# Zeros behind the rows of a sparse expert layer: eight tiles per group, or two row buffers filled once

## What is computed

```python
x = x + attn_a(layernorm(x))   # delta rule, 16 heads of 8, short convolutions
x = x + ffn(layernorm(x))      # 8 experts, the best 2 of each token
x = x + attn_b(layernorm(x))   # linear attention, 16 heads of 8
x = x + ffn(layernorm(x))      # the same experts again
```

```python
probs = softmax(xt @ Wg); topw, topi = top_k(probs, 2); topw = topw / sum(topw)
h = relu(einsum('nd,edf->enf', xt, W1)); y = einsum('enf,efd->end', h, W2)
out = einsum('ne,end->nd', combine, y)   # combine holds topw at topi, else 0
```

## Time and profile before

| | us |
|---|---|
| median of 3 runs | 790.13 |
| lowest and highest | 786.14, 790.35 |
| span of the profiled execution | 951.4 |

### The profile page before, as it was taken

The page is one execution under the profiler, slowest core; times in us unless marked ns, Lnnn a source line. Parts: engine busy times, 40 slices in busy tenths (PEclk is TensorE's granted clock), DMA queues, the critical chain, the costliest instruction groups (busy, mean ns, idle before and its releaser), DMA issues.

```text
span 951.4 us, 17059 instructions
## 1 busy us (share of the span) xinstructions
PE 722.5 (76%) x5202; PEld 588.9 (62%) x5202; DVE 620.4 (65%) x1684; ACT 482.5 (51%) x1270; POOL 479.8 (50%) x550
## 2 busy tenths in 40 slices
PE   5634649888889877878979975798887988199375
PEld 4322428767677756665867865685655868188364
DVE  4789999999999999995754753464434626033224
ACT  4965476979796846474540613243241704054221
POOL 2149896989898989477042033303341122702351
PEclk9865668999999989899875995798777959589697
DMA  5330403040403030103333222234122414335321
GB/s 181 81 81 0 103 11 104 12 114 12 113 11 102 11 103 12 56 1 94 91 97 92 90 68 84 62 89 129 45 87 84 121 45 139 98 101 156 114 73 45
DMA packets 106766, 73.99 MB, mean 78 GB/s; under 512 B 44992, under 2 KB 94656, under 8 KB 106432
## 3 DMA queue, kind: packets, MB, share of 16 engines
q1 hardware_dynamic: 102080, 63.58, 22.8%
q0 software_dynamic: 4608, 9.45, 3.3%
HBM read 45.47 MB, written 27.53 MB: 77 GB/s over the span
## 4 chain that ended last, share of the span: by engine, by line
PE 39%; DVE 27%; issue 13%; another core or an unknown queue 8%; ACT 6%; DMA 3%; POOL 2%; SPq 1%; DVEq 0%; POOLq 0%; ACTq 0%
PE bank L2036 7%; DVE u L2578 6%; PE bank L2122 5%; PE bank L2101 5%; PE bank L2002 5%; DVE hist_mem L2583 4%; DVE hist_mem L2587 4%; DVE prod_mem L2571 3%; PE bank L2092 2%; PE bank L2052 2%; DVE x L2719 2%; PE bank L2040 1%; DMA s_beta<-beta_T 1%; PE bank L1745 1%
## 5 line engine op out<-in xcount | busy, mean ns | idle before, releaser
L1836 PE MATMUL bank<-w,hid 128*128 128x128 f32 x768 | 105.8, 296 | 32.9 <-DVE y_even L2719 17.9
L1836 PEld LDWEIGHTS bank<-w,hid 128*128 128x128 f32 x768 | 99.8, 209 | 44.5 <-issue 13.3
L885 POOL TENSOR_TENSOR oq_mem<-hist_mem,q_t 128x384 f32<-128x384 f32 (+1 forms) x96 | 101.3, 1089 | 0.0
L2578 DVE TENSOR_REDUCE u<-prod_mem 128x32 f32<-128x288 f32 x128 | 86.8, 678 | 3.4
L1175 ACT ACTIVATE hid<-bank 128x512 f32<-128x512 f32 x112 | 62.7, 594 | 50.2 <-PE bank L1816 35.2
L2122 PE MATMUL bank<-w,wv 128*128 x448 | 70.9, 308 | 21.1 <-issue 16.9
L2036 PEld LDWEIGHTS bank<-v_bd,hist_mem 128*64 128x64 f32 x1024 | 74.0, 167 | 17.3 <-issue 17.0
L2036 PE MATMUL bank<-v_bd,hist_mem 128*64 128x18 f32 x1024 | 77.1, 233 | 5.2 <-issue 5.2
L953 POOL DMA_INDIRECT s_xs<-xf,row_at x40 | 39.5, 988 | 81.8 <-DVE row_at L3043 38.1
L2122 PEld LDWEIGHTS bank<-w,wv 128*128 128x128 f32 x448 | 63.8, 218 | 26.3 <-issue 26.1
L1347 ACT ACTIVATE wv<-bank 128x512 f32<-128x512 f32 x56 | 33.7, 602 | 83.7 <-remote 48.6
(11 more groups left out here) (303 smaller groups left out, 1948.6 us busy)
## 6 DMA issues: line engine op xcount, KB each, us to landing
hid<-in_w SPq DMA_DIRECT2D x72, 128.0 KB
s_qkv<-qkv SPq DMA_DIRECT2D x24, 256.0 KB, 3.4
pin<-s_xs SPq DMA_DIRECT2D x76, 64.0 KB
pin<-s_qkv SPq DMA_DIRECT2D x16, 256.0 KB, 2.6
kk<-in_w SPq DMA_DIRECT2D x30, 128.0 KB
s_ys<-q_p SPq DMA_DIRECT2D x28, 128.0 KB
s_ys<-q_t SPq DMA_DIRECT2D x28, 128.0 KB
s_xs<-zeros SPq DMA_DIRECT2D x40, 64.0 KB
```

The lines of the kernel that those rows point to most:

```text
L885: tt(oq[:, :, j, :, 0:HD], s_at, bc(turned[:, n, j], 2, HD), ALU.mult).then_inc(o_part, 1)
L1836: last = nc.tensor.matmul(bank[:, y_bank(e, wide), tokens], hid[:, e % 2, f, tokens], w2[:, e, f], start=(f == 0), stop=(f == FC - 1))
L2578: red(u[:, n], prod[:, n].rearrange("p m e j -> p m j e"), AX_X, ALU.add).then_inc(step, 1)
```

## The change

The group's own row buffers give way to two, `s_rows[0]` and `s_rows[1]`, each large enough for the largest group; group g uses number g % 2. SP fills both with zeros once, in the first layer: sixteen DMAs out of `state`, which is still zero then, four in each of the iterations 0 to 3, as the last thing of the iteration. A tile that reaches past an expert's rows therefore holds zeros, or finite rows that an earlier group left there. `pads` goes, and with it the tile `zeros`, the table of counts `pad_at`, the cast that writes it, and SP's wait for the pads.

Three waits are added. GpSimd's first scatter and VectorE's first sum into `state` wait until all fills have landed. The scatters of groups 2, 3 and 4 wait until TensorE has turned every pair of the groups up to g - 2, the earlier user of the same buffer.

```diff
-        s_xs = [nc.dram_tensor(f"s_xs{g}", [E * ROOM[g], D], F32, kind="Internal").ap() for g in range(len(GROUPS))]
+        s_rows = [nc.dram_tensor(f"s_rows{b}", [E * max(ROOM), D], F32, kind="Internal").ap() for b in range(2)]
+        s_xs = [s_rows[g % 2][0:E * ROOM[g]] for g in range(len(GROUPS))]
...
-        CONSTS, SELECT_OPS, TABLE_OPS = 6 + 2 * len(GROUPS), 8, 20
+        CONSTS, SELECT_OPS, TABLE_OPS = 5 + 2 * len(GROUPS), 8, 19
+        FILLS, FILL_STEPS = E * max(ROOM) * D // (128 * B * H * HV), 4
...
+            def zero_rows(i):
+
+                count = 2 * FILLS // FILL_STEPS
+                for k in range(count * i, count * (i + 1)):
+                    b, at = k // FILLS, k % FILLS
+                    sp.dma_start(s_rows[b].rearrange("(n p q) d -> n p (q d)", n=FILLS, p=128)[at],
+                                 state[:].rearrange("p b h e -> p (b h e)")).then_inc(zeroed, 16)
+
+            sp.wait_ge(pool_ready, POOL_ALL)
             for i in range(NCH - 1):
...
                 if far:
                     load_x(i + 4)
+                if i < FILL_STEPS:
+                    zero_rows(i)
...
-            def pads(g):
-
-                sp.wait_ge(tabled, TABLE_OPS * g + 17)
-                _, starts_at = nc.values_load_multi_w_load_instructions(
-                    pad_at[0:1, g], engines=[mybir.EngineType.SP], min_val=0, max_val=E * ROOM[g] - TILE,
-                    skip_runtime_bounds_check_because=ROWS_WHY)
-                for e in range(E):
-                    sp.dma_start(s_xs[g][bass.ds(starts_at[e], TILE)], zeros[:]).then_inc(padded, 16)
-
             def tile_load(p):
...
-                sp.wait_ge(tabled, TABLE_OPS * g + 17)
+                sp.wait_ge(tabled, TABLE_OPS * g + 16)
...
-                    sp.wait_ge(padded, 16 * E * (g + 1))
...
-            pads(0)
             tile_load(0)
...
-            nc.gpsimd.memset(zeros[:], 0.0).then_inc(consts, 1)
...
                 pool.wait_ge(o_part, NG * GROUP_OPS * NCH)
+                if k == 0:
+                    pool.wait_ge(zeroed, 16 * 2 * FILLS)
+                if g >= 2:
+                    pool.wait_ge(tile_turned, FIRST_TILE[g - 1] // 2)
...
                     dve.wait_ge(numer, J * (c + 1))
+                    if c == 0:
+                        dve.wait_ge(zeroed, 16 * 2 * FILLS)
                     tt(state[:], state[:], dstate, ALU.add).then_inc(state_ready, 1)
...
                 tt(counts, count_at, expert_at[:, g], ALU.subtract).then_inc(tabled, 1)
-                nc.vector.tensor_copy(pad_at[:, g], count_at[one]).then_inc(tabled, 1)
```

More of the change, by code:

```diff
@@ L221, in build @@
         every = sb("every", [128, 128])
-        zeros = sb("zeros", [128, D])
         tile_steps = sb("tile_steps", [128, max(ROOM) // TILE])
@@ L250, in build @@
                  ("started", MOST_TILES * E), ("tile_row", MOST_TILES), ("tile_table", len(GROUPS) * MOST_TILES * 2),
-                 ("pad_at", len(GROUPS) * E), ("tiles", 2 * E), ("first", MOST_TILES), ("expert", MOST_TILES),
+                 ("tiles", 2 * E), ("first", MOST_TILES), ("expert", MOST_TILES),
                  ("offset", MOST_TILES), ("counts", E), ("shift", E)]
@@ L262, in build @@
         tiles, starting, shift = low["tiles"][:, 0:E], low["tiles"][:, E:2 * E], low["shift"]
-        pad_at = low["pad_at"][0:1].bitcast(I32).rearrange("p (g k) -> p g k", g=len(GROUPS))
         BUFFERS = 6
-        ROWS_WHY = "a tile starts inside its expert's room, and a pad starts at an expert's count, which is less than the room by a tile"
+        ROWS_WHY = "a tile starts inside its expert's room"
         EXPERT_WHY = "a tile's expert is the number of experts, of seven, whose tiles start at or below it"
@@ L355, in build @@
         selected, positioned, rows_ready, route_part = sem("selected"), sem("positioned"), sem("rows_ready"), sem("route_part")
-        tabled, padded, combined = sem("tabled"), sem("padded"), sem("combined")
+        tabled, zeroed, combined = sem("tabled"), sem("zeroed"), sem("combined")
         mid_stored, out_stored = sem("mid_stored"), sem("out_stored")
@@ L660, in _ @@
             tile_load(7)
-            pads(1)
             tile_load(8)
@@ L686, in _ @@
             tile_store(13)
-            pads(2)
             tile_load(20)
@@ L713, in _ @@
             tile_load(31)
-            pads(3)
             tile_store(24)
@@ L738, in _ @@
             tile_load(43)
-            pads(4)
             tile_store(35)
@@ L2013, in routed_away @@
                 if full:
-                    pe.wait_ge(tabled, TABLE_OPS * (full - 1) + 2)
+                    pe.wait_ge(tabled, TABLE_OPS * (full - 1) + 1)
             def lin_numer(c, j):
@@ L2106, in tile_up @@
                 k = 2 * p - FIRST_TILE[g]
-                pe.wait_ge(tabled, TABLE_OPS * g + 17)
+                pe.wait_ge(tabled, TABLE_OPS * g + 16)
                 _, experts[p] = nc.values_load_multi_w_load_instructions(
@@ L3067, in table @@
                 tt(counts, count_at, expert_at[:, g], ALU.subtract).then_inc(tabled, 1)
-                nc.vector.tensor_copy(pad_at[:, g], count_at[one]).then_inc(tabled, 1)
                 dve.wait_ge(tabled, base + 1)
                 tt(past[:, :, 0:steps], bc(counts, 2, steps), bc(tile_steps[:, 0:steps], 1, E), ALU.is_gt).then_inc(tabled, 1)
+                dve.wait_ge(tabled, base + 2)
+                red(tiles, past[:, :, 0:steps], AX_X, ALU.add).then_inc(tabled, 1)
                 dve.wait_ge(tabled, base + 3)
-                red(tiles, past[:, :, 0:steps], AX_X, ALU.add).then_inc(tabled, 1)
+                tt(starts, bc(tiles, 1, E), lower[:], ALU.mult).then_inc(tabled, 1)
@@ L3073, in table @@
                 dve.wait_ge(tabled, base + 4)
-                tt(starts, bc(tiles, 1, E), lower[:], ALU.mult).then_inc(tabled, 1)
+                red(starting, starts, AX_X, ALU.add).then_inc(tabled, 1)
                 dve.wait_ge(tabled, base + 5)
-                red(starting, starts, AX_X, ALU.add).then_inc(tabled, 1)
-                dve.wait_ge(tabled, base + 6)
                 tt(started[:, 0:many], bc(number, 2, E), bc(starting[one], 1, many), ALU.is_ge).then_inc(tabled, 1)
                 red(total[:], low["tiles"][one, E - 1:2 * E:E], AX_X, ALU.add).then_inc(tabled, 1)
-                dve.wait_ge(tabled, base + 8)
+                dve.wait_ge(tabled, base + 7)
@@ L3087, in table @@
                 red(first, started[:, 0:many], AX_X, ALU.max).then_inc(tabled, 1)
+                dve.wait_ge(tabled, base + 12)
+                tt(offset, number, first, ALU.subtract).then_inc(tabled, 1)
                 dve.wait_ge(tabled, base + 13)
-                tt(offset, number, first, ALU.subtract).then_inc(tabled, 1)
+                stt(tile_row[:, 0:many], offset, float(TILE), tile_row[:, 0:many], ALU.mult, ALU.mult).then_inc(tabled, 1)
                 dve.wait_ge(tabled, base + 14)
-                stt(tile_row[:, 0:many], offset, float(TILE), tile_row[:, 0:many], ALU.mult, ALU.mult).then_inc(tabled, 1)
@@ L3092, in table @@
-                dve.wait_ge(tabled, base + 15)
                 stt(tile_table[:, g, 0:many, 0], expert, float(ROOM[g]), tile_row[:, 0:many], ALU.mult, ALU.add).then_inc(tabled, 1)
@@ L3099, in back @@
                 rows_of = slice(0, 2 * J * count)
-                dve.wait_ge(tabled, TABLE_OPS * g + 17)
+                dve.wait_ge(tabled, TABLE_OPS * g + 16)
                 dve.wait_ge(route_part, 4 * (k + count))
@@ L3103, in back @@
                    bc(shift, 1, 2 * J * count), ALU.mult).then_inc(tabled, 1)
+                dve.wait_ge(tabled, TABLE_OPS * g + 17)
+                red(row_shift[:, rows_of], sel_shift[:, rows_of], AX_X, ALU.add).then_inc(tabled, 1)
                 dve.wait_ge(tabled, TABLE_OPS * g + 18)
-                red(row_shift[:, rows_of], sel_shift[:, rows_of], AX_X, ALU.add).then_inc(tabled, 1)
-                dve.wait_ge(tabled, TABLE_OPS * g + 19)
                 tt(back_at[:, k:k + count].rearrange("p c s j -> p (c s j)"), row_sum[:, 0:count].rearrange("p c s j -> p (c s j)"),
```

4 lines of the change are left out of this document (2 added, 2 removed).

## The result

| | before | after |
|---|---|---|
| median (lowest to highest), us | 790.24 (786.14 to 799.63), 4 runs | 805.76 (804.09 to 806.66), 4 runs |
| first layer ends at, us in the trace | 435.73 | 456.51 |
| VectorE's waits at `kdot`, us | 3.5 | 22.3 |
| GpSimd's waits for `beta_p`, us | 30.8 | 50.8 |

The changed kernel is slower: ratio 1.0215, 95% interval 1.0181 to 1.0249, so 17 us (14.3 to 19.7). "First layer ends" is the start of its last sum into `o_p` on VectorE. The profiled execution of after took 804.9 us, close to its timed runs; that of before took 951.4 us, and the first experiment shows where the difference lies.

What follows compares the result with a forecast made beforehand. VectorE was taken to bound the first layer, TensorE being busiest in the second. Fills cost 22.3 us, less 2 for pads and 0.3 for casts: +20 us, 790.1 + 20 = 810 us, range 804 to 818, widened 795 to 826.

Steps and rivals of the forecast that it cites:

- The fills stand between s_beta's landing and beta_p's load, and small DMAs wait for them: First layer, SP's queue, chunks 2 to 5: fills priced at their full data time ahead of the pairs.
- Rival B: First layer: small loads overtake the fills or slip between them, only 2 us of gain left, 788 us; chance 0.12.
- 6.55 us a step: First layer: data time of a step's four fills, 2.36 MB at the 360 GB/s of earlier loads.
- Rival C: First layer: stores slower than loads, a step over 10 us; 832 us at 12 us, 863 at the upper bound; chance 0.10.
- the prediction's own formula: First layer: four steps of fill time, less 3.0 us of empty queue and 0.9 us of slack at chunk 5.
- the prediction's 22.3 us: First layer: total cost of the fills, 26.2 less 3.0 less 0.9 us.
- The signs to look for: Changed trace: `kdot` idle 5 to 7 us in chunks 2 to 5, `pairs_in` landing in 8 to 9, first layer ending about 457.
- Pads: 2 us: Second layer: gain from dropping SP's forty pad stores put at 2 us, between 0 and 34.3.
- The margin of 5 to 6 us: Second layer, after `pads(3)`: spare time between the group's first load and TensorE's turn of that tile pair, pads included.
- rival D: Second layer: SP paces it and pads lie on the path; gain up to 34.3 us, time 778, faster from 22.3; chance 0.08.
- The waits added for the shared buffers, and the cast: Second layer: scatter waits cost nothing (tightest margin 13 us, group 3); dropping five casts counted as 0.3 us gained.
- The 161 us between trace and timed runs: Traced span 951.4 against 790.1 us: difference placed in the second layer, the first layer's 22.3 us carried over unscaled.

Runs made afterwards that it cites:

- the first experiment: The kernel before, unchanged, profiled once more: one run of 803.68 us, span 802.0 us.
- fills_after_xr: The changed kernel with each step's four fills moved to the next iteration, behind `load_xr`: 784.27 us, ratio 0.9917 to the kernel before.
- fills_after_pairs: The changed kernel with the fills moved one place, right behind `pairs_in` of the next iteration: 798.44 us, ratio 1.0127 to the kernel before.
- before_again: The kernel before, unchanged, in its second profile: one run of 803.68 us, first layer ending at 436.32 us.
- fills_only: The kernel before, pads kept, plus the sixteen fills at the change's place into two buffers nobody reads: 814.84 us, ratio 1.0298 to the kernel before.
- fills_half: `fills_only` with each fill half as wide (128 x 2304 B): 969.03 us where the kernel before takes 957.04, ratio 1.0142.
- pads_full_2: `fills_after_xr` with the pads and their table entry put back and one more SP wait, rerun on a third chip: 794.03 us, ratio 1.0037 to before.
- fills_after_xr_2: `fills_after_xr` run again on the third chip, as control without pads: 784.33 us, ratio 0.9912 to the kernel before.

## Why the prediction was right

The forecast was 810 us against 805.76 measured, with the sign and the place right. By its own steps:

- *The fills stand between s_beta's landing and beta_p's load, and small DMAs wait for them.* Right: `fills_after_xr` and `fills_after_pairs` have the same traffic and lose nothing, or lose it elsewhere. Rival B, hidden fills, is out. The row that it was read from was thin evidence, though: a 64 KB load issued at 4.11 us, ahead of the 1 MB load, took 4.5 us to land too, so the 5.1 us of the 0.5 KB load don't single out the large one.

```profile
prod_mem<-in_wbeta SPq DMA_DIRECT2D x1, 64.0 KB, 4.5
```

- *6.55 us a step.* Too high: the row taken was that of loads at 360 GB/s, and the fills moved 423 GB/s, 5.6 us a step. Rival C, slow stores, is out by the same rows. With 5.6 us the prediction's own formula gives 4 x 5.6 - 3.0 - 0.9 = 18.5 us, and the waits at `kdot` grew by 18.8. The first layer as a whole grew by 20.2 us (against `before_again`) to 20.8 (against the trace of before); the 1.4 to 2 us that aren't at `kdot` I didn't follow up. By the timed runs the fills at this place cost 23.5 us (`fills_only` against before, and the change against `fills_after_xr`), so the prediction's 22.3 us is near the whole price by luck: too much for the waits it describes, and nothing for another 2 to 4 us, which no run here places and which are no wider than the intervals. The Trainium skill, "DMA: Bandwidth & Descriptors" (section "Anatomy of one DMA — SWDGE (gpsimd) path"), with its 436 GB/s gave an estimate of 5.4 us a step where the fixed part overlaps; its fit is for DMAs from GpSimd and these come from SP, but the trace's 5.6 us agrees with it better than with my row. The 50 us that it gave with the fixed part not overlapped are far from what was measured, and `fills_half` shows a price that follows the bytes.
- *The signs to look for.* `kdot` in chunks 2 to 5: 5.63, 5.27, 4.55, 4.43 us where 5 to 7 were expected, none in later steps. The first layer ends at 456.5 us (457 forecast). One sign was wrong: `pairs_in` was to be issued at the same place and to land in 8 to 9 us. At chunk 2 it was issued 2.2 us later, because the four fills took SP 3.38 us to issue, some 0.85 us each and not 0.4, and its loads landed in 3.9 to 4.0 us (median). The delay is the same, split between issue and landing. That is not harmless: SP's other issues are held too, and that the issue of the fills adds nothing of its own holds only as far as what followed had to wait for their data anyway.
- *Pads: 2 us.* Mis-sized. They were worth 6.5 to 9.7 us by three comparisons (`fills_only` with after, `fills_after_xr` with before, `pads_full_2` with `fills_after_xr_2`), the last of them with the reserve told above. The margin of 5 to 6 us was argued at the first load of one group, from the trace of a chip whose second layer takes 516 us where it takes 356 to 366 with pads on the others; and it left out the loads of `x_b` and the stores behind the pads, and what a gap costs TensorE in clock. This is a piece of rival D: pads on the path, but far from the 22.3 us from which it would decide. D took SP's time for the pads to be the same in the timed runs as in the trace; it wasn't. The five groups take SP 34.3 us there and 21.2 us in `before_again` (3.96, 4.65, 4.61, 4.00 and 3.99), so all of it could not have given 22.3.
- *The waits added for the shared buffers, and the cast.* No wait of theirs shows up: GpSimd's longest wait ahead of a scatter, 17.8 us, is for `row_at`, as in the earlier trace rows, and the next, 17.0 us, is the same in `before_again`.
- *The 161 us between trace and timed runs.* Right to look for them in the second layer, and to carry the first over unscaled: it ends at 435.7 us in one trace and 436.3 in the other.

Put together with what was measured: 790.2 + 23.5 - 6.5 = 807.2 us by the timed runs, and 790.2 + 20.5 - 6.5 = 804.2 with what the first layer shows, against 805.76. The forecast was 4.2 us too high. Most of that is the pads, put at 2 us (2.3 with the cast) and worth at least 6.5; the rest is within the intervals. Its range of 804 to 818 is wider at the top than its own terms make it: fills of 17 to 27 us less 2.3 give 804.8 to 814.8, and the result lies in both.

## What to carry to other kernels

Large transfers that nobody waits for belong at the place in a queue's order where the next small transfer is far off, not where the loop happens to end: here the same 9.4 MB cost 20 us of the first layer in one place and nothing four or five calls further on. Before a DMA is placed, read what is issued behind it on its queue and who waits for that, and price it as its bytes over the rate that large transfers reach. The price of a short stall of TensorE can be the stall and a stretch at the lower clock behind it, so that small delays on a DMA queue in a TensorE-bound stage can be worth more than their own length. Forty small issues that looked like free work were worth 6.5 to 9.7 us here, and an eighth of their bytes cost the same.

## What the hardware showed beyond that

- *SP's issue time isn't constant.* The two `pin` issues take 0.80 us before, 1.33 us behind four half fills and 2.34 us behind four whole ones (chunk 2); a fill's own issue took 0.43 to 1.25 us in the trace of after.
- *These stores are faster than the first loads.* 421 to 425 GB/s at a share of 1.03 to 1.04 with rows of 4608 B and 408 at 1.04 with rows of 2304 B, against 360 GB/s at 1.00 for the mixed loads at the start. Whether it is the direction or the mix of sizes isn't shown.
- *Chips differ.* The same kernel took a median of 789 to 791 us on three occasions and 957.04 us on one chip (952.14 to 969.4, 29 runs). The first layer is the same on all (435 to 438 us where no fill is waited for); the second takes 516 to 521 us on the slow one. In the first trace of before (951.4 us), which is like it, a stretch in which GpSimd issues one indirect DMA after another shows it. The second row is the same part of the program in `before_again`, with GpSimd equally busy:

```profile
702.00:722.00 20.00, 9.15 (x32) 3.74 (x32) 1.69 (x9) 0.71 (x3) 12.95 (x14) 0.66 0.35 108
630.42:650.42 20.00, 20.00 (x227) 17.02 (x228) 12.89 (x50) 5.57 (x15) 12.97 (x14) 1.00 0.73 188
```

TensorE gets 32 matmuls done in 20 us in place of 227, and VectorE and ScalarE do next to nothing. What holds them on that chip isn't shown by any run here.
